# Value products between the first maximum and the second half of a tile's scores: a gated cross-attention block on one core

## The reference, cut to what matters

```python
x = x + tanh(g_xattn) * attention(layernorm(x), ctx)      # x: (32, 56, 128), ctx: (32, 1500, 128), 16 heads of 8
    q, k, v = x @ Wq.T + bq, ctx @ Wk.T + bk, ctx @ Wv.T + bv
    scores = einsum('bhtd,bhcd->bhtc', q, k) / sqrt(8)
    out = einsum('bhtc,bhcd->bhtd', softmax(scores), v) @ Wo.T + bo
x = x + tanh(g_ffn) * ffn(layernorm(x))                    # 160 experts of 64, the 8 largest of each token, and a shared one
```

## Time and profile before

| | us |
|---|---|
| median of 3 runs | 1130.14 |
| lowest and highest | 1128.01, 1133.91 |
| the profiled execution | 1131.5 |
| its span, first to last instruction | 1130.0 |
| TensorE matmuls busy (share of the span) | 1068.0 (95%) |
| TensorE weight loads busy | 707.7 (63%) |
| VectorE busy | 964.1 (85%) |
| ScalarE busy | 847.6 (75%) |
| GpSimd busy | 591.3 (52%) |

### The profile page before, as it was taken

One profiled execution on the slowest core, in us unless ns is written; L12 is line 12 of the kernel. 1 busy time (PEld: TensorE's weight loads), 2 busy tenths in 40 slices (PEclk: granted clock), 3 DMA queues, 4 the chain that ended last, 5 costly groups with the idle time before them and its releaser, 6 DMA issues.

```text
span 1130.0 us, 37375 instructions
## 1 busy us (share of the span) xinstructions
PE 1068.0 (95%) x12122; PEld 707.7 (63%) x12122; DVE 964.1 (85%) x1699; ACT 847.6 (75%) x1817; POOL 591.3 (52%) x984
## 2 busy tenths in 40 slices
PE   2699899999999999999999999988999999999998
PEld 1377677777777777777777777644455555555554
DVE  4688678888888888888888888578999999999998
ACT  2477577777777777777777776587888888888887
POOL 5796888887887887888888887320000000000000
PEclk9899999999999999999999999999999999999999
DMA  7678657667667678577577552473787787787774
GB/s 158 149 171 196 162 132 187 157 141 186 150 158 181 137 171 181 125 184 177 126 184 167 136 144 66 85 203 121 206 234 235 228 225 233 233 236 226 227 236 122
DMA packets 229501, 197.10 MB, mean 174 GB/s; under 512 B 161040, under 2 KB 207264, under 8 KB 229463
## 3 DMA queue, kind: packets, MB, share of 16 engines
q1 hardware_dynamic: 218036, 173.22, 61.2%
q0 software_dynamic: 9200, 21.85, 6.9%
q10 hardware_dynamic: 2226, 1.56, 0.7%
HBM read 109.96 MB, written 12.55 MB: 108 GB/s over the span
## 4 chain that ended last, share of the span: by engine, by line
PE 76%; DVE 12%; issue 4%; SPq 3%; ACT 2%; DMA 1%; POOL 1%; DVEq 0%; POOLq 0%; ACTq 0%
PE bank L1550 15%; PE bank L1540 15%; PE bank L1343 13%; PE bank L1377 11%; PE bank L1358 11%; DVE part_max L1030 6%; PE bank L1413 5%; PE bank L1401 4%; DVE rec L1169 3%; PE bank L1457 1%; DMA ctx_in<-in_ctx_dram 1%; SPq L405 1%; SPq L369 1%; DVE o_raw L1044 1%; DVE ctT L1210 1%
## 5 line engine op out<-in xcount | busy, mean ns | idle before, releaser
L800 ACT ACTIVATE p_exp<-bank 125x448 f32<-125x448 f32 x768 | 400.1, 544 | 190.4 <-PE bank L1358 189.3
L1030 DVE TENSOR_REDUCE part_max<-bank 128x1 f32<-128x500 f32 x672 | 420.2, 671 | 68.0 <-PE bank L1377 67.5
L1358 PE MATMUL bank<-q_st,k_stk 97*125 97x224 f16 x1536 | 273.3, 262 | 7.7 <-issue 4.4
L1377 PE MATMUL bank<-kparts,q_blk 128*128 128x500 f16 x672 | 255.0, 382 | 16.8 <-DVE part_max L1030 14.6
L1358 PEld LDWEIGHTS bank<-q_st,k_stk 97*125 97x125 f16 x1536 | 196.1, 138 | 71.6 <-ACT p_exp L800 13.0
L867 ACT ACTIVATE ctT<-bank 128x448 f32<-128x448 f32 x320 | 173.9, 544 | 43.0 <-DVE v_sb L1203 11.1
L1210 DVE TENSOR_TENSOR ctT<-v_sb,ctT 128x448 f16<-128x448 f32 (+1 forms) x324 | 200.6, 620 | 0.2
L1550 PE MATMUL bank<-ctT,w_ring 128*128 128x448 f16 x816 | 198.7, 352 | 0.1
L1343 PE MATMUL bank<-p_exp,v_sb 125*25 125x168 f32 (+1 forms) x6144 | 187.6, 263 | 0.4 <-ACT p_exp L800 0.4
L874 ACT ACTIVATE ctT<-v_sb 128x448 f16<-128x448 f32 x320 | 182.2, 569 | 3.7 <-DVE v_sb L1203 3.7
L1343 PEld LDWEIGHTS bank<-p_exp,v_sb 125*25 125x25 f32 x6144 | 142.9, 104 | 43.2 <-ACT p_exp L800 0.8
(11 more groups left out here) (191 smaller groups left out, 1373.9 us busy)
## 6 DMA issues: line engine op xcount, KB each, us to landing
k_stk<-kparts SPq DMA_DIRECT2D x384, 93.8 KB, 4.0
v_sb<-c_scratch SPq DMA_DIRECT2D x68, 448.0 KB, 4.4
k_stk<-c_scratch SPq DMA_DIRECT2D x68, 448.0 KB, 4.3
ctx_in<-in_ctx_dram SPq DMA_DIRECT2D x30, 672.0 KB
w_scratch<-w_out POOLq DMA_DIRECT2D x80, 128.0 KB, 3.5
w_in<-in_L_ffn_w_gate_dram POOLq DMA_DIRECT2D x80, 64.0 KB, 3.7
w_in<-in_L_ffn_w_down_dram POOLq DMA_DIRECT2D x80, 64.0 KB, 4.2
v_sb<-c_scratch SPq DMA_DIRECT2D x8, 336.0 KB, 3.9
```

The lines of the kernel that those rows point to most:

```text
L800: act.activation(p_exp[0:KP, j % PR, f * 448:(f + 1) * 448], ST[f][0:KP, 0:448], ACT.Exp).then_inc(exp_done, 1)
L1030: v.reduce_max(part_max[:, i // NCH, i % NCH:i % NCH + 1], SM[i % NSM][:, 0:CK], axis=AX.X).then_inc(sm_maxed, 1)
L1358: last = pe.matmul(ST[f][0:KP, (g % 2) * GC:(g % 2 + 1) * GC], k_stk[0:97, u, g, j * KP:(j + 1) * KP], q_st[0:97, u, g, :, :].rearrange("p ...
L1377: pe.matmul(SM[i % NSM][:, 0:CK], rows, kparts[:, u, 0, c * CK:(c + 1) * CK], start=True, stop=True).then_inc(sm_done, 1)
```

## The change

The value block of odd rounds moves from behind the second scores to between the first maximum of the round and the second scores:

```diff
                     for f in range(2):
+                        if f == 1 and values_there and jv % 2:
+                            value_product(bv_, jv - 1)
+                            value_product(bv_, jv)
                         if scores_there:
                             scores(bs, js, f)
                         for i in chunks_at(k, 0) if f == 0 and on(step, 1) else []:
                             maxima(step, i)
-                    if values_there and jv % 2:
-                        value_product(bv_, jv - 1)
-                        value_product(bv_, jv)
                     for i in chunks_at(k, 1) if on(step, 1) else []:
                         maxima(step, i)
```

## The result

| | before | after |
|---|---|---|
| median us, in the same comparison | 1129.35 | 1163.58 |
| ratio, 95% interval | | 1.0272 [1.0231, 1.0313] |
| the profiled execution, us | 1131.5 | 1166.43 |
| its span, us | 1130.0 | 1164.9 |

The change makes the kernel slower. The ratio and its interval leave out one disturbed run, which the median of after still holds. By the ratio the change costs 0.0272 × 1129.35 = 30.7 us (26 to 35); between the two profiled executions it is 34.9.

A forecast was written before the change was run, and what follows sets the result against it. TensorE sets the pace. Rounds 1, 3, 5 and 9 (1.08 us) plus round 11 (0.20) give 1.28 us a step, times 31 steps +39.7 us: 1170 us predicted, 3.5% slower, range 1146 to 1191.

The forecast's parts named there:

- Where the wait is: Even rounds' second scores wait for the exponential on their PSUM bank: trip 1.04 us, TensorE work 0.87, lack 0.17.
- Entering the block from a maximum, 0.09: Join into the value block, now behind a maximum: taken to cost 0.09 us, as it does behind scores.
- "faster" rival: Entry behind a maximum is free: each of 192 blocks saves 0.09, 17 us, to about 1113; chance 0.06.
- Late weights, 0.05 behind the block and 0.05 behind the wait: Scores behind the block or behind a wait start with weights not loaded ahead: +0.05 us each.
- Rounds 1, 3, 5 and 9 at 0.27: Blocks that nothing hides pay 0.05 + 0.17 + 0.05 = 0.27 us each, 1.08 in a step.
- Round 7 hidden: Round 7's 0.27 us goes into the round 8 maximum's wait for VectorE: cost 0.
- VectorE's wait takes only round 7's 0.27: Round 8's maximum waits 0.60 us for VectorE (28 waits, 16.9 us); the sum let it hide only round 7's 0.27.
- the low end of the range: 1146 us: free block entry saves 15 us, the rest of round 8's wait hides 8 us more, rounded down.
- Round 11 at 0.34 without the projection: Only the transpose follows round 11 there: lack 0.24, cost 0.34 us; with the projection 0.05; mean 0.20.
- Nothing in the last steps: Last attention steps without maxima: TensorE waits for the exponentials already, so no cost was counted.
- the high end: 1191 us: longer trips 11 us, round 7 not hidden 8 us, and 2 for the last steps.
- The expectation of 25 to 45 us for weight loads behind exponentials: Score weight loads (line 1358) waiting for exponentials (line 800) rise from 7.1 us to 25 to 45, in about 150 places.

The follow-up runs named there:

- e9: e7 with the second maximum of rounds 2, 4 and 6 also moved ahead of their second scores: 1140.40 us, ratio 1.0088 to the kernel before.
- e3: Kernel before, with the value block moved ahead of the second scores in rounds 1, 3, 5 and 9 only: 1156.04 us, ratio 1.0216.
- e4: Kernel before, with the value block moved ahead of the second scores in round 7 only: 1133.47 us, ratio 1.0018.
- e6: Kernel before, with the second maximum of round 8 moved behind that round's value chunk: 1117.61 us, ratio 0.9862.
- e7: Changed kernel, with the second maximum of round 8 moved behind that round's value chunk: 1155.97 us, ratio 1.0208 to the kernel before.

## Why the prediction was right

The forecast was 1170 us, slower; measured were 1163.58, and 1160.1 by the ratio (1.0272 × 1129.35). The cause is the one forecast; its size was put at 39.7 us and is 30.7, and about half of the difference comes from a gain that no part of the sum had.

- **Where the wait is: right.** It is at the second scores of the even rounds, behind their own bank's exponential, and the expectation of 1.04 us from scores to scores is met (421.00 to 422.04). e9 shows the cause by filling the trip.
- **Entering the block from a maximum, 0.09: right.** 0.30 from the maximum to the block against 0.21 or 0.22 to other work. The free entry, on which the "faster" rival rested, does not exist. The Trainium skill's "TensorEngine Tiling (Array Packing)", Key Properties, by which a change of the tiling mode drains the engine, names no neighbour, and the 0.30 here agrees with that; no row shows a drain by itself.
- **Late weights, 0.05 behind the block and 0.05 behind the wait: right.** Both are 0.24 in place of 0.19 (421.00 to 421.24, 422.04 to 422.28). The rule of the Trainium skill's "TensorE: Matmul & The Clock Gate", Architectural detail, that weight loads can be pulled ahead of matmuls in flight, would have taken the first away; behind this block the trace does not show it.
- **Rounds 1, 3, 5 and 9 at 0.27: right in the trace.** 0.05 + 0.17 + 0.05 is read from the rows above (0.26 with the unrounded steps); e3 puts the four at 24.4 / 31 / 4 = 0.20. In its trace each costs 0.26 or 0.27 (3.53 us from round 1 to round 3, as with the whole change), and the maximum of round 8 waits 0.30 less in the steps with the projection, as described below.
- **Round 7 hidden: right.** e4 costs 2.0 us, where the bare block would be 8.
- **VectorE's wait takes only round 7's 0.27: wrong, the largest error of the sum.** I took one wait of 0.60, a mean over 28, and left the rest of it to the low end of the range. It has two sizes. Before, VectorE's multiplication in the normalisation (line 1173) and TensorE's second scores of round 8, then the same and the maximum in a step in which the projection has just run:

```profile
407.21 0.39 DVE L1173 TENSOR_TENSOR o_nrm<-rec,o_raw 128x224 f32<-128x224 f32 x1
407.64 0.36 PE L1358 MATMUL bank<-q_st,k_stk 97*125 97x224 f16 x2
...
428.28 0.69 DVE L1173 TENSOR_TENSOR o_nrm<-rec,o_raw 128x224 f32<-128x224 f32 x1
428.71 0.35 PE L1358 MATMUL bank<-q_st,k_stk 97*125 97x224 f16 x2
...
429.62 0.38 PE L1377 MATMUL bank<-kparts,q_blk 128*128 128x500 f16 x1 [0.55 <-DVE part_max L1030]
```

After, a step of either kind:

```profile
425.30 0.39 DVE L1173 TENSOR_TENSOR o_nrm<-rec,o_raw 128x224 f32<-128x224 f32 x1
425.94 0.40 PE L1358 MATMUL bank<-q_st,k_stk 97*125 97x224 f16 x2
426.34 0.39 PE L1377 MATMUL bank<-kparts,q_blk 128*128 128x500 f16 x1
...
447.55 0.39 DVE L1173 TENSOR_TENSOR o_nrm<-rec,o_raw 128x224 f32<-128x224 f32 x1
448.19 0.41 PE L1358 MATMUL bank<-q_st,k_stk 97*125 97x224 f16 x2
448.59 0.39 PE L1377 MATMUL bank<-kparts,q_blk 128*128 128x500 f16 x1
```

Before, the maximum starts 0.91 us behind the scores where the projection has run (428.71 to 429.62) and 0.61 in the other steps (407.64 to 408.25; its weight load is in the earlier trace rows); after, 0.40 in both. So in every other step 0.30 more is given back than I counted, 0.15 us in the mean. That 0.30 is the length of one VectorE instruction, 0.69 in these steps before and 0.39 in the others and after. The move shifted it against GpSimd's work (see the last section). Nothing in the forecast had that; it was luck, and so in part is that the result lies under 1170. The transposes say the same: a step grew by 1.20 us without the projection (20.27 to 21.47) and by 0.89 with it (21.36 to 22.25). e6 and e7 take the wait away, and the change then costs more, 38.4 us; that this is near the 39.7 of the sum is chance, as round 7 pays in it and round 11 less than I had put.

- **Round 11 at 0.34 without the projection: wrong.** It is 0.13 in every step, and the second scores of round 0 waited for their exponential before the change too. I had read ScalarE's order in round 5 only, and not the key copy of round 11. That takes the mean from 0.20 to 0.13.
- **Nothing in the last steps: not refuted.** The 1.9 us between the two traces are within what that part differs from trace to trace; 2 had been named in the high end.

Put together from the trace: 4 × 0.26 + 0.13 − 0.15 = 1.02 us in a step, 31.6 us over 31 steps, where the transposes show 32.4. The expectation of 25 to 45 us for weight loads behind exponentials was too low (55.0, in 146 places where 150 were named), for the reason that e9 gave; that of under 10 for maxima behind VectorE held (6.4).

## What to carry to other kernels

Before moving a block in an engine's order, list the buffers it stands between, and for each the trip through the other engine and the work left between two uses without the block: what is missing is paid in each round (here 1.04 − 0.87). A wait for a third engine later in the loop swallows part of such a loss, so read that wait in each kind of step, not as a mean, and look at the length of the instruction that ends it: it can change when the engines shift. It is also the first thing to move: one maximum put behind work that hardly had to wait gave 1.4%, where every move of the large block lost.

## What was not expected of the hardware

VectorE's multiplication at line 1173 took 0.39 us each of the 113 times in the eleven traces that no GpSimd instruction was running when it started. With one running, as far as GpSimd's rows tell, which are rough, it took 0.50 or more in 125 of 239. No run moved GpSimd's work alone, so the rows show that the two go together, and not how one holds up the other.

From the start of the value block to the work behind it there are 0.90 us if that is scores or a maximum (420.10 to 421.00; weights of 125 or 128 columns), but 0.79 if it is the transpose (412.82 to 413.61), whose weights are 7 columns wide. That the columns are the reason is not shown, as the transpose differs in other ways too.

The idle of the block's own weight loads, "issue" with 40.6 us in 134 places (0.30 each), is not time lost in that size: the join into the block costs 0.09.
